# A graph layer pair on one core: raw rows of every second group gathered ahead, starting in the prepare block

## The reference

```python
h = relu(layernorm(x))
Wh = h @ W + b                               # layer 1
Wr, Wc = Wh[src], Wh[dst]
sim = sum(Wr * Wc) / max(|Wr| * |Wc|, 1e-8)
base = edge_weight * softplus(deg_coeff[0] * edge_weight_n2 + deg_coeff[1]) * (src != dst)
pos = segment_sum((base * relu(sim))[:, None] * Wc, src)
neg = segment_sum((base * -relu(-sim))[:, None] * Wc, src)
x = x + scale * (c0 * pos + c1 * neg + c2 * Wh)               # c = softmax, scale = softplus
h = relu(layernorm(x))
msgs = mlp(concat(h[dst], h[src]))           # layer 2
agg = segment_sum(msgs, dst)
x = x + mlp(concat(h, agg))
```

## Time and profile before

| | us |
|---|---|
| median of the runs | 2582.36 |
| lowest, highest of three | 2574.97, 2586.78 |
| the profiled execution | 2563.28 |
| its span, first to last instruction | 2561.5 |
| busy in it: PE, DVE, ACT, POOL | 1723.2, 1549.9, 848.9, 1599.2 |
| scatters of edge layer 1, x392, busy | 628.8 |
| gathers of edge layer 1, x296, busy | 289.5 |

### The profile page before, as it was taken

The page is one execution under the profiler, slowest core; times in us unless marked ns, Lnnn a source line. Parts: engine busy times, 40 slices in busy tenths (PEclk is TensorE's granted clock), DMA queues, the critical chain, the costliest instruction groups (busy, mean ns, idle before and its releaser), DMA issues. The chain is left out here.

```text
span 2561.5 us, 52835 instructions
## 1 busy us (share of the span) xinstructions
PE 1723.2 (67%) x13575; PEld 1408.5 (55%) x13575; DVE 1549.9 (61%) x5934; ACT 848.9 (33%) x3238; POOL 1599.2 (62%) x1364
## 2 busy tenths in 40 slices
PE   3664766666666666676660038787778777877999
PEld 2444656666656566565650026666656666666444
DVE  6884756666666666566664935554544445456677
ACT  3772323323223232232322722222222222222665
POOL 5884888888888888888887654444444444441333
PEclk9986555555555555555555558887888788788999
DMA  3774544544445445454533753333323323331676
GB/s 116 257 246 135 119 86 84 91 90 86 92 81 94 84 90 92 85 92 82 91 49 90 248 147 92 73 81 72 75 71 80 71 72 72 76 78 29 198 210 188
DMA packets 355054, 273.07 MB, mean 107 GB/s; under 512 B 94672, under 2 KB 298528, under 8 KB 354976
## 3 DMA queue, kind: packets, MB, share of 16 engines
q1 hardware_dynamic: 271530, 233.22, 31.1%
q0 software_dynamic: 81536, 38.61, 14.2%
q10 hardware_dynamic: 1910, 0.37, 0.1%
HBM read 206.69 MB, written 65.34 MB: 106 GB/s over the span
## 5 line engine op out<-in xcount | busy, mean ns | idle before, releaser
L1290 POOL DMA_INDIRECT x<-e_sums,e_to x392 | 628.8, 1604 | 146.1 <-issue 115.1
L934 POOL DMA_INDIRECT e_near_source<-h,e_near_ids x392 | 388.3, 990 | 450.9 <-DVE e_near_ids L947 320.4
L1527 PE MATMUL bank<-e_window,e_onehot 128*128 128x64 f32 x2352 | 526.8, 423 | 167.2 <-DVE e_onehot L1315 132.0
L1527 PEld LDWEIGHTS bank<-e_window,e_onehot 128*128 128x128 f32 x2352 | 509.0, 331 | 186.3 <-issue 126.3
L1044 PE MATMUL bank<-e_near_to_edge,e_near_window 128*64 128x128 f32 x2352 | 219.1, 296 | 255.7 <-DMA e_near_window<-h 149.3
L1265 POOL DMA_INDIRECT e_ends<-wh,e_ids x296 | 289.5, 978 | 101.2 <-issue 100.9
L1575 PE MATMUL bank<-e_parts,e_same 128*128 128x64 bf16 x2940 | 177.5, 241 | 230.7 <-DVE e_parts L1384 129.4
L1044 PEld LDWEIGHTS bank<-e_near_to_edge,e_near_window 128*64 128x64 f32 x2352 | 166.5, 151 | 291.9 <-DVE e_near_to_edge L955 149.4
L1575 PEld LDWEIGHTS bank<-e_parts,e_same 128*128 128x128 bf16 x2940 | 166.5, 131 | 249.2 <-issue 249.2
L1017 ACT ACTIVATE e_near_hid<-bank,mb_col 128x512 f32<-128x512 f32 x98 | 67.3, 687 | 628.4 <-PE bank L1064 379.4
L968 DVE TENSOR_TENSOR e_near_msgs<-bank,mb_row 128x256 f32<-128x256 f32 x98 | 41.3, 421 | 322.9 <-PE bank L1072 209.3
(11 more groups left out here) (173 smaller groups left out, 3301.5 us busy)
## 6 DMA issues: line engine op xcount, KB each, us to landing
e_window<-wh SPq DMA_DIRECT2D x392, 96.0 KB
e_near_window<-h SPq DMA_DIRECT2D x392, 96.0 KB
e_owners<-ends SPq DMA_DIRECT2D x98, 256.0 KB
n_x<-x SPq DMA_DIRECT2D x98, 256.0 KB, 3.1
n_x<-in_x_dram SPq DMA_DIRECT2D x49, 256.0 KB
wh<-n_wh SPq DMA_DIRECT2D x49, 256.0 KB
x<-n_x SPq DMA_DIRECT2D x49, 256.0 KB
e_rel<-rel SPq DMA_DIRECT2D x98, 128.0 KB
```

The costliest lines, as they stand in the source:

```text
L934: pool.indirect_dma_start(out=t.source[s][:, j, :], out_offset=None, in_=tabs["h1"], in_offset=bass.IndirectOffsetOnAxis(ap=t.ids[s][:, j: ...
L1290: pool.indirect_dma_start(out=added_tab, out_offset=bass.IndirectOffsetOnAxis(ap=t.to[s][:, j:j + 1], axis=0), in_=t.sums[s][:, j, :], in_ ...
L1527: last = nc.tensor.matmul(bank[FIND_BANKS[s]][:, j * D:(j + 1) * D], onehot, window, start=w == 0, stop=w == WK - 1)
```

## The change

- Raw groups are now the groups 3, 5, 7, ..., 95: 47 groups, 188 rows. In the edge layer the even groups and the groups 1 and 97 are gathered, 204 gathers, two a step.
- The first 14 raw rows are issued in the prepare block. For that the loads of src have a semaphore of their own, VectorE casts and TensorE turns src first, and the copy to `edge_i` comes right behind. 98 rows follow two behind each centring of node stage 0, and the last 76 in pairs after the last centring.
- The raw group's norm has two sets of buffers, its mean is no longer an instruction of its own, and its parts run in every second step instead of every fourth. The bank on TensorE stays one.
- In layer 1's edge loops one round more is unrolled.

```diff
-AHEAD = ESLOTS - 1
-AHEADS = GROUPS // ESLOTS
+AHEAD_FIRST, AHEAD_EVERY = 3, 2
+EARLY = 14
+AHEADS = (GROUPS - 1 - AHEAD_FIRST) // AHEAD_EVERY
+def gather_ahead(pool, c, x, start, end):
+    for n in range(start, end):
+        pool.indirect_dma_start(
+            out=c["ahead"][:, n // G, n % G, :], out_offset=None, in_=x,
+            in_offset=bass.IndirectOffsetOnAxis(
+                ap=c["edge_i"][:, 0, AHEAD_FIRST + AHEAD_EVERY * (n // G), n % G:n % G + 1], axis=0),
+        ).then_inc(c["ahead_in"], 16)
# prepare, gpsimd
+                pool.wait_ge(src_taken, 1)
+                for n in range(0, EARLY, 2):
+                    pool.sem_inc(src_paced, 1)
+                    gather_ahead(pool, c, x, n, n + 2)
# prepare, vector
-                dve.wait_ge(rows_loaded, 12 * 16)
-                for i in range(2):
-                    steps.mark(nc.vector.tensor_copy(rows_f[:, i, 0:FULL, :], rows_i[:, i, 0:FULL, :]))
+                dve.wait_ge(src_loaded, 3 * 16)
+                nc.vector.tensor_copy(rows_f[:, 0, 0:FULL, :], rows_i[:, 0, 0:FULL, :]).then_inc(src_ready, 1)
...
+                dve.wait_ge(cols_done, 1)
+                nc.vector.tensor_copy(flat(c["edge_i"][:, 0, 0:GROUPS, :]), c["bank"][0][:, 0:TC]).then_inc(src_taken, 1)
+                dve.wait_ge(rows_loaded, 9 * 16)
# node stage 0, gpsimd
-        gather_ahead(0, 6)
         for n in range(BLOCKS):
             ln.pool_centre(pool, n % SLOTS, n // SLOTS)
-            gather_ahead(6 + 8 * n // 5, 6 + 8 * (n + 1) // 5)
-        gather_ahead(6 + 8 * BLOCKS // 5, len(rows_ahead))
+            gather_ahead(pool, c, x, EARLY + 2 * n, EARLY + 2 * (n + 1))
+        for n in range(EARLY + 2 * BLOCKS, AHEADS * G, 2):
+            pool.sem_inc(paced, 1)
+            gather_ahead(pool, c, x, n, n + 2)
# edge layer 1, gpsimd
-            share = AHEAD * G // ESLOTS
-            for n in range(share * s, G * (s + 1) if last else share * (s + 1)):
-                gather_rows(n // G, k, n % G)
+            for n in range(2 * s, 2 * s + 2):
+                gather_rows(AHEAD_EVERY * (n // G), k, n % G)
+            if s % AHEAD_EVERY and not t.is_ahead(s, k, near):
+                for j in range(G):
+                    gather_rows(s, k, j)
# edge layer 1, vector: the raw group's norm
-            nc.vector.tensor_scalar(a.mean[:], a.total[:], 1.0 / D, None, ALU.mult).then_inc(a.mean_ready, 1)
-            nc.vector.tensor_tensor(a.split(a.xc), a.row(k), a.by_row(a.mean), ALU.subtract).then_inc(a.xc_ready, 1)
+            nc.vector.scalar_tensor_tensor(a.split(xc), a.by_row(total), -1.0 / D, a.row(s, k, 0),
+                                           ALU.mult, ALU.add).then_inc(a.xc_ready, 1)
```

More of the change, by code:

```diff
@@ L438, in rounds_of_blocks @@
         steps(k)
-    with eng.Fori(first, full) as k:
+    with eng.Fori(first, full - plain) as k:
         steps(k)
-    for k in range(full, full + first + 1):
+    for k in range(full - plain, full + first + 1):
         steps(k)
@@ L557, in node_phase0 @@
     SPLIT = R // 2 + 1
-    pads_stored = slots.sem("pads_stored")
+    pads_stored, paced = slots.sem("pads_stored"), slots.sem("paced")
     turn_bank, wh_bank = c["bank"][0:2], c["bank"][2:4]
@@ L611, in gpsimd @@
     def gpsimd(pool):
-        rows_ahead = [(g, j) for g in range(AHEADS) for j in range(G)]
-        def gather_ahead(start, end):
-            for g, j in rows_ahead[start:end]:
-                pool.indirect_dma_start(
-                    out=c["ahead"][:, g, j, :], out_offset=None, in_=x,
-                    in_offset=bass.IndirectOffsetOnAxis(ap=c["edge_i"][:, 0, ESLOTS * g + AHEAD, j:j + 1], axis=0),
-                ).then_inc(c["ahead_in"], 16)
-        gather_ahead(0, 6)
         for n in range(BLOCKS):
             ln.pool_centre(pool, n % SLOTS, n // SLOTS)
-            gather_ahead(6 + 8 * n // 5, 6 + 8 * (n + 1) // 5)
-        gather_ahead(6 + 8 * BLOCKS // 5, len(rows_ahead))
+            gather_ahead(pool, c, x, EARLY + 2 * n, EARLY + 2 * (n + 1))
+        for n in range(EARLY + 2 * BLOCKS, AHEADS * G, 2):
+            pool.sem_inc(paced, 1)
+            gather_ahead(pool, c, x, n, n + 2)
         all_stored(pool)
@@ L1129, in bufs @@
             return slots.bufs(name, shape, ESLOTS, dt)
+        self.plain = 1 - layer
         self.src_at = layer
@@ L1197, in end_rows, with is_ahead @@
         return self.ends[s][:, j, end, :]
-    def is_ahead(self, s, near):
-        return near and self.layer == 0 and s == AHEAD
+    def is_ahead(self, s, k, near):
+        among = not isinstance(k, int) or 0 <= ESLOTS * k + s - AHEAD_FIRST < AHEAD_EVERY * AHEADS
+        return near and self.layer == 0 and s % AHEAD_EVERY == AHEAD_FIRST % AHEAD_EVERY and among
     def all_gathered(self, eng, s, k, near):
-        if self.is_ahead(s, near):
-            eng.wait_ge(self.ahead.copied, k + 1)
+        if self.is_ahead(s, k, near):
+            eng.wait_ge(self.ahead.copied, self.ahead.nth(s, k, AHEAD_FIRST) + 1)
             return
-        eng.wait_ge(self.gathered[s], 16 * G * (1 if near else 2) * (k + 1))
+        times = 1 if near and self.layer == 0 and s % AHEAD_EVERY else k + 1
+        if near and self.layer == 0 and s % AHEAD_EVERY and k:
+            times = 2
+        eng.wait_ge(self.gathered[s], 16 * G * (1 if near else 2) * times)
 def same_block(j, i):
@@ L1292, in scatter @@
                 in_=t.sums[s][:, j, :], in_offset=None, compute_op=ALU.add).then_inc(t.added[s], 16)
-    rounds_of_blocks(pool, [(0, gather), (-3, scatter)], ESLOTS, GROUPS)
+    rounds_of_blocks(pool, [(0, gather), (-3, scatter)], ESLOTS, GROUPS, t.plain)
     for s in range(ESLOTS):
@@ L1442, in found @@
             act.wait_ge(t.ends_used, count(s, k, ESLOTS, ESLOTS))
-        if t.is_ahead(s, near):
-            act.wait_ge(t.ahead.wh_done, k + 1)
+        if t.is_ahead(s, k, near):
+            act.wait_ge(t.ahead.wh_done, t.ahead.nth(s, k, AHEAD_FIRST) + 1)
             nc.scalar.copy(t.ends[s][:, :, t.src_at, :],
```

121 lines of the change are left out of this document (68 added, 53 removed).

## The result

After took 2607.4 us (median of 5 runs, 2603.3 to 2618.5), before 2582.4 (5 runs, 2568.6 to 2589.0): ratio 1.0112, 95% interval 1.0071 to 1.0153. It is slower by 25 us by the medians and 29 by the ratio, where the sum had 14 less, and just inside the range. The profiled execution of after has 2603.3 us (span 2601.5), 40 us above before's; 25.7 of them stand before the last scatter of edge layer 1, the rest in stages that the change does not touch.

What follows compares the result with a forecast made beforehand. POOL's issue of indirect DMAs was taken as the bound. First gather +77, layer start -12, fewer gathers -117 and late landing +38 gave -14: 2549 profiled, 2568 us as median, range 2530 to 2608.

Steps and rivals of the forecast that it cites:

- First node stage, 49 x 3.47: Node stage 0: 49 blocks of one centring and two raw rows at POOL's 3.47 us each, 170 us.
- the short form: First node stage: a centring and two rows take POOL 3.46 us when it did not wait for the mean.
- my bound of 194: First node stage: upper bound of 49 x 3.96 = 194 us, 24 us above the value taken.
- the long form: First node stage: rival with centrings of 1.58 beside DVE's passes, 3.96 us a block; +24, 2592, no change; chance 0.15.
- Prepare, 32.7 for the first centring: Prepare block: 14 raw rows go out in POOL's idle gap, so the first centring starts at 32.7 instead of 36.4.
- Start of the layer, -12: Edge layer start: first gather to first scatter takes 20 us instead of 32.3; bounds 15 and 32.
- Tail, 95 us and 2 for odd issues: Behind the last centring: 76 remaining raw rows take POOL 95 us, plus about 2 for odd late issues.
- Steady layer, -117 + 38 = -79: Edge layer: 92 fewer gathers save 117 us; scatters landing 0.4 us late over 94 steps cost 38.
- both rivals on it: Edge layer: landing never late, 2530 us, chance 0.19; or another engines' ring bounding the steps, 2618 us, 0.16.
- One in eight is late: Edge layer before the change: one step in eight has its first scatter waiting for the previous group's landing.
- the ring: Edge layer: rival, a DVE-PE-ACT loop through the raw group's norm replaces POOL as bound; 11.15 us a step, 2618, chance 0.16.
- a first gather beyond 315: Sign of being wrong: the edge layer's first gather coming later than 315 us, where 300 was forecast.

Runs made afterwards that it cites:

- act_mean: After with the first node stage's row mean made by ScalarE instead of VectorE; ratio 1.0076 against before.
- after_mean: After with the row mean made by VectorE's two-source scalar_tensor_tensor instead of tensor_scalar; ratio 1.0093 against before.
- order: After with the row mean on ScalarE and VectorE's pass over x moved to the end of its step; ratio 1.0061 against before.
- early0: After with no raw rows in the prepare block, two behind each centring and 90 behind the last; 2621.7 us, single run.
- memset_tail: After with the last 76 raw-row gathers replaced by 76 POOL memsets, so 19 groups read zeros; 2551.6 us, single run.
- extra_gather: After with one further row gather, its data unused, in each step of edge layer 1; 2687.8 us, single run.

## Why the prediction was wrong

By the profiled pair the last scatter came 25.7 us later where the sum had -14. The 40 us between these two, part by part:

- **First node stage, 49 x 3.47: the largest miss, 16.6 us.** From the first centring to the 49th and its block it took 182.7 + 3.85 = 186.6, not 170. The argument, that DVE has about 2.7 us a block against POOL's 3.46, "so means are ready and I take the short form", ignored that DVE and POOL hold each other. I had the sign of it in the earlier trace rows, a centring of 1.58 beside DVE's pass, and read it as what happens only when POOL has waited. The short form's rows (38.63, 42.09) stand in the stage's first blocks, where the pass over x has not begun. Before's trace has two-row blocks of both prices further on, where all parts run:

```profile
62.85 1.06 POOL L511 TENSOR_TENSOR n_xc<-n_x,n_mean 128x512 f32<-128x512 f32 x1
...
65.34 1.37 POOL L616 DMA_INDIRECT ahead<-in_x_dram,edge_i  x1 [0.30 <-issue]
66.73 1.05 POOL L511 TENSOR_TENSOR n_xc<-n_x,n_mean 128x512 f32<-128x512 f32 x1
...
112.23 1.05 POOL L511 TENSOR_TENSOR n_xc<-n_x,n_mean 128x512 f32<-128x512 f32 x1
...
115.67 1.05 POOL L511 TENSOR_TENSOR n_xc<-n_x,n_mean 128x512 f32<-128x512 f32 x1
```

The first takes 3.88 with a gather of 1.37, the second 3.44. So 3.47 was possible with every part at work, but only while no gather started inside the pass; with two rows in each block POOL and DVE fell into one phase and every block had the long gather. That the holding sets the interval is shown in part: POOL's row adds up to it in after and in act_mean, the mean alone was not it (after_mean), taking one instruction away gave 0.14 and moving the other 0.07 more (act_mean, order), the last mixed with the clock. The price (186.6) lies inside my bound of 194, but for another reason than the long form.

- **Prepare, 32.7 for the first centring: 3.0 us.** early0, a single run, gives 32.27, so the removed work was costed rightly; what I priced at nothing, 14 rows beside one-time code, was not free.
- **Start of the layer, -12: 14.7 us.** 34.65 instead of 20. "Labels, windows and the first finds are ready while POOL is still issuing raw rows" is the step that failed. memset_tail has 23.8: 10.9 us are the crawl beside the tail's rows. The other 3.8 are not taken apart; the crawl beside the layer's own 12 gathers and my low guess for two steps of DVE and PE are both in them.
- **Tail, 95 us and 2 for odd issues:** 98.1, from 222.3 to 320.4, with one hole of 3.3 us at 240.7. The rows themselves were right.
- **Steady layer, -117 + 38 = -79:** first to last scatter went from 1120.4 to 1046.3, so -74.2. The wait of 0.4 us was 0.37, and extra_gather shows its cause. This step held, both rivals on it fell: landing is late, and no ring closed. Most of the 5 us stand in the first eight steps (11.1 in the mean). "One in eight is late" can't be read from the earlier trace rows: in before 11 of the 98 groups had over 0.5 us idle ahead of their first scatter, in after 56.
- Of the rivals the ring has the nearest time, 2618, and did not happen: the layer kept the forecast pace. The long form (chance 0.15, stage of 194, 2592) has the nearest mechanism, centrings and gathers beside DVE's passes; its result was "no change", and the measured ratio lies above 0.5%. That 2607 lies in the range is luck: the range was drawn for landing and ring, and the miss came from the first stage and the start of the layer. One sign of being wrong that the prediction named did come, a first gather beyond 315.

From the last scatter of the layer to the end the profiled after took 1200.2 us against 1185.9 in before; kernels here that are identical from there on have 1174 to 1207, so the 14 us say nothing of the change.

## What to carry to other kernels

Moving an issue from a saturated queue to another stretch where the same queue is saturated saves nothing, and can lose the cover it gave to a wait. A steady price must be read from many blocks in which every part of the pipeline runs, and where they have two prices, ask what decides between them and how the change moves it. And when a queue's idle time is filled with gathers, ask what one-time code the other engines run beside it: here 14 rows were nearly free in the prepare block, and 12 behind the last centring cost 9 us.
